# Row maxima of an attention unit: one transposing matmul to eight rows, spread over the queries by VectorE with a constant 0/1 tile

## The reference

```python
xn = layernorm(x)                        # x: 8 x 2048 x 1024
q, k, v = split(xn @ W_attn + b_attn)    # 16 heads of 64
att = q k^T / (8 * temperature) + slope_h * (key - query), causal
y = softmax(att) v @ W_proj + b_proj
h = silu(xn @ wg^T) * (xn @ wu^T)        # 3072 wide, int8-like weights / 127
out = x + y + h @ wd^T
```

## Time and profile before

| what | value |
|---|---|
| median of 3 runs | 1156.49 us (1156.03 to 1157.23) |
| profiled execution, own time | 1156.21 us |
| its span on the slowest core (core 4) | 1154.7 us |
| spans of the eight cores | 1150.5 to 1154.7 us, granted clock 0.995 to 0.999 of full speed |
| PE / DVE / ACT / POOL busy | 96 / 51 / 46 / 23% of the span |

### The profile page before, as it was taken

How to read it: one execution, slowest core, us unless ns; L and a number is a source line. 1 busy time by engine, 2 the same in 40 slices (tenths; PEclk the granted TensorE clock), 3 DMA queues, 4 the chain that set the end, 5 groups by cost and what they waited for, 6 DMA issues and landing times.

```text
span 1154.7 us, 24726 instructions; the slowest of 8 cores (1150.5 to 1154.7 us)
## 1 busy us (share of the span) xinstructions
PE 1107.8 (96%) x7830; PEld 569.8 (49%) x7830; DVE 586.5 (51%) x1190; ACT 531.3 (46%) x965; POOL 267.2 (23%) x289
## 2 busy tenths in 40 slices
PE   2898999999999999999999999999999999999998
PEld 1344455555555555555555555555555344444443
DVE  5441866766666766676666666666773100000110
ACT  1443456655755665565566566556667300000000
POOL 7210122222221222122222112112223432121221
PEclk9899999999999999999999999999999999999999
DMA  9439041333312333133311312112420652525222
GB/s 188 126 95 179 12 80 41 75 66 70 74 29 62 78 62 65 38 74 67 69 38 24 67 33 52 31 31 56 165 56 20 217 189 73 182 73 182 73 73 73
DMA packets 39648, 94.19 MB, mean 82 GB/s; under 512 B 5876, under 2 KB 26485, under 8 KB 38438
## 3 DMA queue, kind: packets, MB, share of 16 engines
q0 software_dynamic: 7872, 35.66, 16.1%
q1 hardware_dynamic: 28770, 48.45, 13.5%
q10 hardware_dynamic: 2884, 8.50, 1.9%
HBM read 90.49 MB, written 27.26 MB: 102 GB/s over the span
## 4 chain that ended last, share of the span: by engine, by line
PE 88%; DVE 5%; issue 3%; DMA 2%; ACT 1%; POOL 1%; DVEq 0%; ACTq 0%; POOLq 0%; SPq 0%
PE ps_gu L727 25%; PE ps_dn L895 14%; PE ps_s L818 10%; PE ps_t L799 10%; PE ps_m L707 9%; PE ps_y L834 5%; PE ps_dn L890 5%; PE ps_t L767 5%; DVE cm L548 3%; DMA xstage<-xin 2%; PE ps_m L847 1%; PE ps_s L821 1%; PE ps_t L803 1%; PE ps_m L855 1%; DVE st L496 1%
## 5 line engine op out<-in xcount | busy, mean ns | idle before, releaser
L548 DVE TENSOR_REDUCE cm<-ps_s 128x1 f32<-128x512 f32 (+3 forms) x640 | 380.1, 608 | 198.5 <-PE ps_s L818 105.0
L656 ACT ACTIVATE pt<-ps_t 128x512 bf16<-128x512 f32 (+1 forms) x576 | 327.3, 575 | 222.3 <-PE ps_t L799 134.2
L727 PE MATMUL ps_gu<-xnT,wubuf 128*128 128x512 bf16 x768 | 261.9, 378 | 2.1 <-DVE hst L484 1.7
L727 PE MATMUL ps_gu<-xnT,wgbuf 128*128 128x512 bf16 x768 | 261.3, 378 | 1.2 <-ACT kst L600 1.2
L818 PE MATMUL ps_s<-kx,qx 67*128 67x512 bf16 (+3 forms) x640 | 213.1, 347 | 10.4 <-DVE cm L548 9.1
L799 PE MATMUL ps_t<-qx,kx 98*128 98x512 bf16 (+3 forms) x640 | 216.4, 348 | 1.5 <-ACT pt L656 1.2
L426 POOL TENSOR_SCALAR th_s<-th_s 128x512 f32<-128x512 f32 x96 | 59.4, 618 | 626.0 <-ACT th_s L608 626.0
L895 PE MATMUL ps_dn<-wdres,hb 128*128 128x512 bf16 x768 | 168.5, 379 | 0.0
L834 PEld LDWEIGHTS ps_y<-Vt,pt 128*128 128x128 bf16 x2176 | 125.4, 97 | 82.0 <-issue 0.4
L834 PE MATMUL ps_y<-Vt,pt 128*128 128x65 bf16 x2176 | 138.9, 193 | 0.0
L589 DVE SCALAR_TENSOR_TENSOR outsb<-ps_dn,xres 128x512 f32<-128x512 f32 x32 | 20.7, 687 | 205.3 <-PE ps_dn L895 205.3
(11 more groups left out here) (77 smaller groups left out, 793.1 us busy)
## 6 DMA issues: line engine op xcount, KB each, us to landing
h_sc<-hst SPq DMA_DIRECT2D x96, 128.0 KB, 1.7
hb<-h_sc SPq DMA_DIRECT2D x4, 3072.0 KB, 14.1
xstage<-xin SPq DMA_DIRECT2D x16, 512.0 KB, 6.3
xres<-xin POOLq DMA_DIRECT2D x16, 512.0 KB, 4.6
out<-outsb ACTq DMA_DIRECT2D x15, 512.0 KB, 2.7
wgbuf<-wg_r POOLq DMA_DIRECT2D x12, 512.0 KB, 6.4
wubuf<-wu_r POOLq DMA_DIRECT2D x12, 512.0 KB, 9.1
wd_sc<-wd_r POOLq DMA_DIRECT2D x12, 512.0 KB, 8.3
```

What stands on the lines that cost most here:

```text
L548: e.tensor_reduce(cm[:, c0:c0 + 1], ps_s[:, s % 2 * 512:s % 2 * 512 + w], AX.X, AluOpType.max, negate=True).then_inc(sem["v_mx"], 1)
L656: e.activation(pt[t % NPT][:, 0:w], ps_t[:, t % 2 * 512:t % 2 * 512 + w], AF.Exp).then_inc(sem["a_e"], 1)
L727: mm = e.matmul(ps_gu[:, r // 8 * 512:r // 8 * 512 + 512], w[:, w0:w0 + 128], xnT[:, dc * T + tb * 512:dc * T + tb * 512 + 512], start=(dc ...
```

## The change

The four transposing matmuls of a unit become one. Its eight columns (head and rest of four query blocks) go to rows 96 to 103 of `ps_m`, 128 wide. VectorE then writes rows 96 to 103 of `qx`, 512 wide: the 128 columns read four times, times a constant tile of zeros and ones in which rows 96+2i and 97+2i are one over the i-th 128 queries. `kx` has ones in all eight rows. The copy by ScalarE goes. The contraction of the key groups grows from 98 to 104 rows. One more constant (8 x 512 bf16) is loaded on ScalarE's queue. The plan of steps is the same.

```diff
-KT = 98
+KT = 104
+    tiles = din("tiles", [8, 512], BF16)
+        tile_s = sb(st, "tile_s", [128, 512], BF16)
-        nm = [sb(st, f"nm{i}", [128, 4 * KT], BF16) for i in range(2)]
+        nm = [sb(st, f"nm{i}", [128, KT], BF16) for i in range(2)]
-                m_users.append(("a_m", M[1] + 1))
+                m_users.append(("v_m", M[1] + 1))
-                    e.memset(kx[q][j][96:98, :], 1.0).then_inc(sem["g_set"], 1)
+                    e.memset(kx[q][j][96:KT, :], 1.0).then_inc(sem["g_set"], 1)
-                    e.wait_ge(sem["l_const"], 16 * 4)
+                    e.wait_ge(sem["l_const"], 16 * 5)
 # VectorE, at a unit's last score group
-                        n3 = nm[par].rearrange("p (i c) -> p i c", c=KT)
+                        n3 = nm[par][:, 96:KT].rearrange("p (i c) -> p i c", c=2)
-                        e.tensor_copy(n3[:, :, 96:97], src).then_inc(sem["v_mc"], 1)
+                        e.tensor_copy(n3[:, :, 0:1], src).then_inc(sem["v_mc"], 1)
 # VectorE, behind the reductions and the copy of q of step k, ahead of the product of gate and up
+                if M is not None and M[0] == "m":
+                    n = M[1]
+                    h, b = n // 4, n % 4
+                    e.wait_ge(sem["p_m"], n + 1)
+                    e.tensor_tensor(
+                        qx[h // 2 % 2][h % 2][96:KT, b * 512:(b + 1) * 512].rearrange("p (i q) -> p i q", i=4),
+                        ps_m[96:KT, 0:128].unsqueeze(1).broadcast_to([8, 4, 128]),
+                        tile_s[96:KT, :].rearrange("p (i q) -> p i q", i=4), AluOpType.mult).then_inc(
+                            sem["v_m"], 1)
 # ScalarE
-                if M[0] == "m":
-                    n = M[1]
-                    h, b = n // 4, n % 4
-                    e.wait_ge(sem["p_m"], n + 1)
-                    e.activation(qx[h // 2 % 2][h % 2][96:98, b * 512:(b + 1) * 512], ps_m[96:98, :],
-                                 AF.Copy).then_inc(sem["a_m"], 1)
 # TensorE
-                        e.wait_ge(sem["a_m"], n + 1)
+                        e.wait_ge(sem["v_m"], n + 1)
-                    for i in range(4):
-                        mm = e.matmul(ps_m[0:KT, i * 128:(i + 1) * 128], nm[n % 2][:, i * KT:(i + 1) * KT],
-                                      ident_s[:, :], start=(i == 0), stop=(i == 3))
-                    mm.then_inc(sem["p_m"], 1)
+                    e.matmul(ps_m[0:KT, 0:128], nm[n % 2][:, :], ident_s[:, :], start=True,
+                             stop=True).then_inc(sem["p_m"], 1)
+    tiles = np.repeat(np.repeat(np.eye(4, dtype=np.float32), 2, axis=0), 128, axis=1)
```

More of the change, by code:

```diff
@@ L42 @@
     "g_set", "g_th", "g_s", "g_xr",
-    "v_t", "v_cbq", "v_ln", "v_xn", "v_q", "v_mx", "v_mc", "v_rc", "v_y", "v_h", "v_out",
-    "a_c", "a_sd", "a_xe", "a_v", "a_k", "a_m", "a_e", "a_yt", "a_th", "a_g", "a_b",
+    "v_t", "v_cbq", "v_ln", "v_xn", "v_q", "v_mx", "v_mc", "v_m", "v_rc", "v_y", "v_h", "v_out",
+    "a_c", "a_sd", "a_xe", "a_v", "a_k", "a_e", "a_yt", "a_th", "a_g", "a_b",
     "p_c", "p_xT", "p_v", "p_qk", "p_s", "p_m", "p_t", "p_av", "p_yt", "p_g", "p_u", "p_b", "p_d", "p_dl",
@@ L567, in _ @@
                             e.wait_ge(sem["p_m"], n - 1)
-                        e.tensor_copy(n3[:, :, 96:97], src).then_inc(sem["v_mc"], 1)
+                        e.tensor_copy(n3[:, :, 0:1], src).then_inc(sem["v_mc"], 1)
                         e.wait_ge(sem["v_mc"], c + 1)
-                        e.tensor_tensor(n3[:, :, 97:98], src, n3[:, :, 96:97], AluOpType.subtract).then_inc(
+                        e.tensor_tensor(n3[:, :, 1:2], src, n3[:, :, 0:1], AluOpType.subtract).then_inc(
                             sem["v_mc"], 1)
@@ L614, in _ @@
             for dst, src in ((onesf_s[:, :], ones_f[:, :]), (temp_s[:, :], temp[:, :]),
-                             (bqk_s[:, :], battn_qk[:, :]), (mask_s[:, :], masks[:, :])):
+                             (bqk_s[:, :], battn_qk[:, :]), (mask_s[:, :], masks[:, :]),
+                             (tile_s[96:KT, :], tiles[:, :])):
                 e.dma_start(out=dst, in_=src).then_inc(sem["l_const"], 16)
@@ L661, in _ @@
                     continue
-                if M[0] == "m":
-                    n = M[1]
-                    h, b = n // 4, n % 4
-                    e.wait_ge(sem["p_m"], n + 1)
-                    e.activation(qx[h // 2 % 2][h % 2][96:98, b * 512:(b + 1) * 512], ps_m[96:98, :],
-                                 AF.Copy).then_inc(sem["a_m"], 1)
-                elif M[0] == "yt":
+                if M[0] == "yt":
                     n = M[1]
@@ L939, in _consts @@
         "masks": masks.astype(BF),
+        "tiles": tiles.astype(BF),
         "slopes": np.ascontiguousarray(np.stack(parts, axis=1)),
```

## The result

The changed kernel took 1153.22 us in the median against 1156.53 us of the kernel before; the ratio is 0.9969 with a 95% interval of 0.9957 to 0.9981, so 3.6 us less (2.2 to 5.0). The ratio leaves out one of the six executions of the changed kernel, which took 1186 us with a granted clock of 0.956 to 0.975 on four of the cores. The profiled execution took 1153.88 us.

The account below looks back on a forecast made before the run. The prediction took TensorE to bound the attention stage, nine tenths of its chain of waits, with VectorE next. It summed 1156.2 - 11.3 + 5.6 + 1.0 = 1151.5 us, 1151.8 us on the median's scale, range 1146.3 to 1157.3.

Parts of the forecast that it names:

- Three matmuls are worth 11.3 us: TensorE in the attention stage: three of four transposing matmuls go in 64 units, saving 11.3 us (10.6 to 11.5).
- ScalarE gives nothing: ScalarE in the attention stage: removing its 64 copies, 37.8 us of work, gains 0 (bounds 0 and 1.2 us).
- 0.35 us at each b = 3: Score matmuls behind the product wait for VectorE's reductions: 0.35 us at each of sixteen units, 5.6 us (1.6 to 13.6).
- No loss at b = 0, 1, 2: At these units beyond the head, VectorE's product delays reductions without TensorE losing time: 0 us, read from unit 18.
- The next user of `ps_m` comes no sooner: PSUM bank of the transposition: its next user comes no sooner than the first key group, so the product stays hidden.
- The first key group is hidden, key matmuls wait nowhere for the product: Key matmuls come two steps or more behind the transposition; the product ends 0.8 to 1.2 us behind it, no wait.
- The head: 1.0 us of stall: Units 0 to 2, at the attention stage's head: VectorE's product costs 0.33 us each, 1.0 us together (0 to 2.3).
- The product: 0.68 us and 0.05 to 0.15 us around it: VectorE's new product takes 0.68 us (0.60 to 0.81), 44 us in all, with 0.05 to 0.15 us between instructions.
- The other signs: VectorE busy up 44 us, ScalarE down 38, score matmuls' waits for VectorE about 15 us, attention stage ending near 889.
- Rival C: VectorE becomes the bound around each b = 3 unit: 0.85 us at all sixteen, head 2.3; 1161.1 us; chance 0.10.
- Rival A: VectorE's delay in the attention stage is absorbed nearly everywhere: stalls 1.6 us, total 1146.8 us; chance 0.22.
- rival B: The swap is even: sixteen b = 3 units pay 0.6 us each, the head 1.5 us; 1156.3 us; chance 0.22.

Follow-up runs that it names:

- e2: Kernel before, with one transposing matmul, ScalarE copying its 128 columns four times, no VectorE product, position bias zero; score stage 769.2 us against 777.5.
- e1: Kernel before, four transposing matmuls kept, VectorE instead of ScalarE writing the rows of the maxima; score stage 780.0 us, 2.5 us above before.
- e10: Kernel before, with VectorE's cast of the four maxima replaced by a reduction that writes bf16; score stage 776.4 us, 1.1 less than before.
- e9: Changed kernel, with VectorE's cast of the four maxima replaced by a reduction that writes bf16; score stage 771.3 us, ratio to the kernel before 0.9960.
- e6: Changed kernel, with VectorE's product made twice at each unit, the first time into a scratch tile; score stage 797 us against 773.1.
- e4: Changed kernel, with VectorE's product one step later at units with b = 3; score stage 779.8 us, ratio to the kernel before 1.0032.
- e7: Changed kernel, with VectorE's product at partition 0 into a scratch tile, maxima rows left at one, position bias zero; score stage 768.6 us.
- e11: Changed kernel, but four matmuls and ScalarE's copy at b = 3 and units 0 to 2, reduction for the cast; 1146.21 us, ratio to before 0.9918.
- e3: Changed kernel, with ScalarE writing the eight rows in four scaled instructions of 128 columns at all units, no VectorE product; score stage 780.8 us.

## Why the prediction was right, point by point

The forecast was 1151.8 us within 1146.3 and 1157.3; measured 1153.2. For the stage it made 4.7 us less (11.3 - 5.6 - 1.0), measured 4.3. The direction, the main place of the loss and its price hold. Two terms were far off and nearly cancelled, the matmuls by 3.0 us and ScalarE by 2.1 us, and two waits that the prediction held for hidden are there; that the sum is so near owes something to luck. The terms as measured do not add up to 4.3 us exactly, since e2 and the stalls count some places twice: at units 16, 30 and 48 the time that e2 loses in a wait for ScalarE comes back when the copy is gone.

- **Three matmuls are worth 11.3 us.** Mis-sized: e2 shows 8.3 us. The rate was nearly right (0.165 to 0.168 us a unit for 0.176), the step from rate to time was not: at about a fifth of the units TensorE runs into a wait for another engine behind the "m", and the saved time is spent there. The 81 ns for a matmul of 128 columns that the Trainium skill has ("TensorE: Matmul & The Clock Gate", section "Back-to-back issue gap") are not seen: three less give 0.165 us, 55 ns each.
- **ScalarE gives nothing** (bounds 0 to 1.2 us). Wrong: e1 gains 0.66, 0.79, 0.48, 0.28 and 0.22 us at units 16, 20, 30, 48 and 56. With 0.32 us of unit 20's taken off for the cast (e10) this is 2.1 us. I had read the four waits of key matmuls for the exponential as the whole of ScalarE's hold on TensorE; the chain at unit 16 has the copy on it.
- **0.35 us at each b = 3.** Right: +0.17 and +0.18 us at units 7 and 27 is 0.35 less the 0.17 saved, and 5.9 us for the fifteen stands against the 5.6; single units go from 0.13 to 0.89. Unit 11 was forecast at 0.85 us and measured 0.72 + 0.17 = 0.89. I had put 0.53 us of that down to its long cast; in e9, where no cast is long, it still pays 0.44 + 0.17 = 0.61, so the cast was worth 0.28: the subtraction behind it, 0.18 us before, is then drawn out to 0.43. Unit 15 (0.72) is an exception without a long cast; its score matmul lay 0.27 us behind the reduction before, where others have 0.57 and more.
- **No loss at b = 0, 1, 2.** Right in sum, wrong at the unit it was read from. At unit 18 I put the product ahead of both reductions that begin at 327.18. By the order of VectorE's work it stands behind the first of the two, and the changed kernel has it there (slowest core, start us, us, engine):

```profile
329.41 0.68 DVE L550 TENSOR_REDUCE cm<-ps_s 128x1 f32<-128x512 f32 x1
...
330.12 0.70 DVE L580 TENSOR_TENSOR qx<-ps_m,tile_s 8x512 bf16<-8x512 f32 x1
...
331.07 0.38 PE L859 MATMUL ps_m<-ident_s,ysb 128*128 128x128 bf16 x4 [0.18 <-issue]
```

  The score matmuls lose nothing, as forecast, but the transposition of y two steps later, the next user of `ps_m`, starts 0.25 us behind the product's end and is 0.33 us late against e2; the unit's stretch is 0.32 us longer than before. In e6, where the product is later still, that gap is 0.25 us at five units, and there the list names the product as what was waited for five times. "The next user of `ps_m` comes no sooner" fails here.
- **The first key group is hidden, key matmuls wait nowhere for the product.** Wrong. The product was to end 0.8 to 1.2 us behind the matmul; at unit 27 it ends 2.2 us behind it (448.12 to 450.28), and the key matmul of three steps later, at 450.42, is held by it. At all fourteen units with b = 3 from 7 to 59, and at units 0 and 1, the key matmul starts 0.14 or 0.15 us behind the product. The prediction had named this as a sign of being wrong. It cost little beside the wait for the reduction behind it, which was forecast; e4 shows what it costs when the product comes later.
- **The head: 1.0 us of stall.** Too low: 1.6 us, which is 1.1 us net of the matmuls.
- **The product: 0.68 us and 0.05 to 0.15 us around it.** 0.70 us, and a gap of 0.03 us on both sides for an overlap of 0.08 us; at unit 27 the reduction moved by 0.81 us for the 0.78 put. e7 shows that 0.23 us of a stall is what the partition costs.
- **The other signs.** VectorE's busy sum rose by 41.4 us (forecast 44) and ScalarE's fell by 36.6 (38); the stage ended at 889.3 us (889). The listed wait of score matmuls is 10.1 us and not 15; the chain, whose share of VectorE's reductions grew by 6 us, has what the list leaves out.

Rival C had the right price for unit 11, and nearly for 15, but not for sixteen. Rival A, by which the delay is absorbed, is refuted by the b = 3 units; rival B by the other 45.

Not settled: the 0.37 us at unit 16 in e11 has no experiment of its own.

## What to carry to other kernels

When work moves off the bounding engine, charge the receiving engine not by its mean load but at the steps where its queue has two deadlines: here the units with b = 3 and the head gave back more than half of what the matmuls brought, and the old way for just those nearly doubled the gain of the stage. A product put later to spare one consumer must be timed against all others: here the key matmul, and the next user of the PSUM bank that it reads. An instruction at partition 96 between neighbours at 0 cost VectorE about 0.2 us more than at 0, and its duration hardly shows it; price it from the starts, not from the busy time.

## What the runs showed of the hardware that I had not expected

- VectorE's overlap of 0.08 us between neighbours turns into a gap of 0.03 us in front of and behind an instruction at partition 96, also with waits already met; worth 4.6 us here (e7). Between two instructions at partition 96 the overlap is there (e6).
- A cast of 4 numbers a partition took up to 1.17 us in place of 0.17, ending 0.03 us behind a GpSimd operation that ran when it began; a reduction that writes bf16 took 0.16 to 0.18 us at all units (e9, e10). The Trainium skill, "SBUF — State Buffer", section "Who interferes with whom", tells of an exclusive pair of ports that such a copy and GpSimd share; the trace agrees.
- ScalarE took 349 ns for 8 x 128 with a scale from SBUF (e3), 590 ns for 8 x 512 without one (e2).
